# A cross-attention stage written out in 16 steps, with every value product inside its own step and eight places for probabilities

## The reference

```
q = (x @ Wq)        # 2048 rows, 8 heads of 64
k = (context @ Wk)  # 1601 rows
v = (context @ Wv)
scores = einsum('bhnd,bhmd->bhnm', q, k) * 64 ** -0.5
attn = softmax(scores, axis=-1)
out = einsum('bhnm,bhmd->bhnd', attn, v)
x = layernorm(x + out @ Wo + bo)
```

## Time and profile before

| what | us |
|---|---|
| median of 3 runs | 970.12 (964.15, 970.12, 972.71) |
| the profiled execution's own time | 970.8 |
| its span, first to last instruction | 969.0 |
| PE busy | 903.2 (93%) |
| POOL busy | 591.4 (61%) |
| DVE busy | 554.7 (57%) |
| ACT busy | 351.0 (36%) |
| granted TensorE clock, mean | 0.978 |

### The profile page before, as it was taken

One profiled execution on the slowest core, in us unless ns is written; L12 is line 12 of the kernel. 1 busy time (PEld: TensorE's weight loads), 2 busy tenths in 40 slices (PEclk: granted clock), 3 DMA queues, 4 the chain that ended last, 5 costly groups with the idle time before them and its releaser, 6 DMA issues. The chain is left out here.

```text
span 969.0 us, 14096 instructions
## 1 busy us (share of the span) xinstructions
PE 903.2 (93%) x4616; PEld 536.6 (55%) x4616; DVE 554.7 (57%) x1123; ACT 351.0 (36%) x493; POOL 591.4 (61%) x397
## 2 busy tenths in 40 slices
PE   6989699999999999999999999989799999989993
PEld 2655354555465455455445455445478888855552
DVE  3897457568557568557557748653645221235562
ACT  3244144434325444425344425433241211124342
POOL 0463198898777889778789769874104500028885
PEclk9999799999999999999999999989899999999997
DMA  9013300000001000001000001040497100323310
GB/s 281 19 46 111 98 1 1 22 1 1 1 1 45 22 1 2 1 1 44 22 1 1 1 1 44 1 153 1 120 321 260 60 22 22 112 83 109 97 37 17
DMA packets 42877, 52.92 MB, mean 55 GB/s; under 512 B 4400, under 2 KB 33856, under 8 KB 42816
## 3 DMA queue, kind: packets, MB, share of 16 engines
q1 hardware_dynamic: 35808, 44.21, 14.4%
q0 software_dynamic: 3744, 6.32, 2.0%
q10 hardware_dynamic: 3264, 1.57, 0.6%
HBM read 38.42 MB, written 17.59 MB: 58 GB/s over the span
## 5 line engine op out<-in xcount | busy, mean ns | idle before, releaser
L625 POOL TENSOR_TENSOR accG<-accG,probs 128x1024 f32<-128x1024 f32 (+1 forms) x170 | 403.5, 2374 | 39.9 <-ACT probs L658 22.7
L658 ACT ACTIVATE probs<-st 128x1024 f32<-128x1024 f32 (+1 forms) x208 | 211.3, 1025 | 239.1 <-PE st L854 150.3
L712 DVE TENSOR_REDUCE mxp<-mx 128x1 f32<-128x512 f32 x360 | 231.2, 686 | 92.2 <-PE mx L839 89.3
L883 PE MATMUL av<-probs,V 128*64 128x512 f32 (+1 forms) x832 | 192.4, 600 | 0.0
L839 PE MATMUL mx<-K_hi,Q_hi 64*128 64x512 f32 (+1 forms) x480 | 165.4, 404 | 4.7 <-DVE mxp L712 4.7
L854 PE MATMUL st<-Q_hi,K_lo 64*128 64x512 f32 (+1 forms) x416 | 127.0, 408 | 0.0
L854 PE MATMUL st<-M,ones_r 64*128 64x512 f32 (+1 forms) x416 | 123.5, 403 | 0.0
L854 PE MATMUL st<-Q_hi,K_hi 64*128 64x512 f32 (+1 forms) x416 | 98.8, 447 | 12.7 <-ACT probs L658 12.7
L883 PEld LDWEIGHTS av<-probs,V 128*64 128x64 f32 (+1 forms) x832 | 54.1, 136 | 98.2 <-issue 83.0
L839 PEld LDWEIGHTS mx<-K_hi,Q_hi 64*128 64x128 f32 x480 | 76.1, 184 | 53.1 <-DVE mxp L712 28.5
L854 PE MATMUL st<-Q_lo,K_hi 64*128 64x512 f32 (+1 forms) x416 | 86.4, 395 | 0.0
(11 more groups left out here) (198 smaller groups left out, 1240.1 us busy)
## 6 DMA issues: line engine op xcount, KB each, us to landing
w_gate_up<-in_gate_up SPq DMA_DIRECT2D x4, 2048.0 KB, 20.2
w_down<-in_down SPq DMA_DIRECT2D x2, 2048.0 KB, 15.6
xs<-scratch_sorted_x SPq DMA_DIRECT2D x31, 128.5 KB, 2.1
scratch_sorted_x<-zero SPq DMA_DIRECT2D x7, 514.0 KB, 8.0
xT<-in_xT SPq DMA_DIRECT2D x4, 512.0 KB, 8.0
xring<-in_x SPq DMA_DIRECT2D x4, 512.0 KB, 8.6
scratch_x1b<-xT SPq DMA_DIRECT2D x4, 512.0 KB, 2.9
x<-scratch_x1b SPq DMA_DIRECT2D x4, 512.0 KB, 3.9
```

The source lines that it names most:

```text
L625: pool.tensor_tensor(accG[0:r], so_far[0:r], probs[0:r, (p * KT + t) % RING], ALU.add).then_inc(g_add, 1)
L658: act.activation(probs[0:r, s], st[g % 2][0:r, :], ACT.Exp, scale=DH ** -0.5).then_inc(a_probs, 1)
L712: dve.tensor_reduce(mxp[:, par, h * QT + i, j:j + 1], mx[h][:, 0:kn], AX.X, ALU.max).then_inc(v_mx, 1)
L883: mm = pe.matmul(av[h * DH:(h + 1) * DH, :], V[0:r, t, (2 * p + h) * DH:(2 * p + h + 1) * DH], probs[0:r, g % RING, h * QC:(h + 1) * QC], ...
```

## The change

The attention stage is rewritten; the other stages are untouched. On every engine the 16 steps are written out (`for S in range(STEPS)`), and the loops, the counts from registers and the semaphore increments and same-engine waits that served them are gone. What else differs:

- PE takes the tiles in four runs, `RUNS`: tiles 0 to 2, 3 to 5, 6 to 8, 9 to 12. After each run come the values of its own tiles, so all 13 values are in their own step, and tiles 0 and 1 are done whole.
- Where a piece stands in a tile is a table, `PIECE_AT`: for each tile, after how many parts the piece of the first and of the second head comes. Tile 0 has none. The last two pieces stand behind tile 12.
- `sums` of the step before comes after the first run. `accG` is two tensors in turn, so that POOL's first addition waits for the sums of two steps before.
- `RING` is 8. `DIVIDE_AFTER` is (10, 10, 16, 16).
- ACT copies `av` (`copy_av`) ahead of `Q_hi`.

```diff
-DIVIDE_AFTER = (8, 8, 18, 18)
-RING = 4
+RUNS = (range(0, 3), range(3, 6), range(6, 9), range(9, KT))
+PIECE_AT = {1: (4, 4), 2: (4, 4), 3: (0, 2), 4: (1, 3), 5: (3, 4), 6: (0, 2), 7: (1, 3), 8: (3, 4),
+            9: (0, 2), 10: (1, 3), 11: (2, 4), 12: (3, 4)}
+DIVIDE_AFTER = (10, 10, 16, 16)
+RING = 8
...
-        accG = sb("accG", [P, 2 * QC])
+        accG = [sb(f"accG{i}", [P, 2 * QC]) for i in range(2)]
...
+                    if n == 0:
+                        at_least(pool, p_sum, S - 1)
+                        so_far = probs[:, place(S, 0)]
...
+            for S in range(STEPS):
+                c, p = divmod(S, PAIRS)
+                if S > 0:
+                    copy_av(S - 1)
+                if S + 1 < STEPS:
+                    q_high(S + 1)
+                for t in range(KT):
+                    exp(S, t)
+                    if p == 1 and t == NORM_AFTER and c > 0:
+                        norm(c - 1)
...
+                if n > 2:
+                    pe.wait_ge(v_mx, (F - 1) * PIECES + n - 2)
...
+            def tile(S, t, first_piece):
+
+                at_least(pe, a_probs, S * KT + t - 1)
+                for slot in range(4 if first_piece is None else 5):
                     for h in range(2):
-                        score(c, p, t, part, h)
...
+                        if first_piece is None or slot < PIECE_AT[t][h]:
+                            score(S, t, slot, h)
+                        elif slot == PIECE_AT[t][h]:
+                            piece(S + 1, first_piece + h)
+                        else:
+                            score(S, t, slot - 1, h)
...
-            chunk(0, True, False)
-            with pe.Fori(1, CHUNKS - 1) as c:
-                chunk(c, False, False)
-            chunk(CHUNKS - 1, False, True)
-            values(CHUNKS - 1, PAIRS - 1, KT - 1)
+            for S in range(STEPS):
+                c, p = divmod(S, PAIRS)
+                ahead = S + 1 < STEPS
+                max_transpose(S)
+                if ahead:
+                    q_proj(S + 1)
+                n = 1
+                for run in RUNS:
+                    for t in run:
+                        tile(S, t, n if ahead and t in PIECE_AT else None)
+                        n += 2 if t in PIECE_AT else 0
+                    if run is RUNS[0] and S > 0:
+                        sums(S - 1)
+                    if run is RUNS[-1]:
+                        if ahead:
+                            piece(S + 1, n)
+                            piece(S + 1, n + 1)
+                        if p == 0 and c > 0:
+                            output(c - 1)
+                    for t in run:
+                        values(S, t)
             last_output(False)
```

More of the change, by code:

```diff
@@ L523, in rows_of, with place @@
             return P if t < KT - 1 else LAST
[L528 to L540, removed]
+        def place(S, t):
+            return (S * KT + t) % RING
         def piece_of(n):
@@ L551, in _ @@
         def _(sp):
[L552 to L572, removed]
+            x1_tiles = io["x1b"].rearrange("(t p) n -> p t n", p=P)
@@ L609, in inverse @@
                 pool.tensor_tensor(shift3[:], nmean3[:], rstd3[:], ALU.mult).then_inc(g_shift3, 1)
[L611 to L630, removed]
+            for S in range(STEPS):
+                c, p = divmod(S, PAIRS)
+                total = accG[S % 2]
+                shared = LAST_V if S == STEPS - 1 else ()
+                for n, t in enumerate(t for t in range(1, KT) if t not in shared):
+                    if p == 1 and n == 0 and c > 0:
+                        inverse(c - 1)
+                    r = rows_of(t)
+                    pool.wait_ge(a_probs, S * KT + t + 1)
+                    if n == 0:
+                        at_least(pool, p_sum, S - 1)
+                        so_far = probs[:, place(S, 0)]
+                    else:
+                        pool.wait_ge(g_add, S * G_ADDS + n)
+                        so_far = total
+                    pool.tensor_tensor(total[0:r], so_far[0:r], probs[0:r, place(S, t)], ALU.add).then_inc(g_add, 1)
@@ L693, in _ @@
+            copy_av(STEPS - 1)
         @block.vector
         def _(dve):
[L695 to L717 removed]
@@ new lines, in _ @@
+            for i in range(DIVS):
+                divide(STEPS - 2, i)
+            for n, t in enumerate(LAST_V):
+                r = rows_of(t)
+                dve.wait_ge(a_probs, (STEPS - 1) * KT + t + 1)
+                part = probs[0:r, place(STEPS - 1, t)]
+                if n == 0:
+                    dve.tensor_copy(accL[:], part).then_inc(v_add, 1)
+                else:
+                    dve.wait_ge(v_add, n)
+                    dve.tensor_tensor(accL[0:r], accL[0:r], part, ALU.add).then_inc(v_add, 1)
@@ L810, in _ @@
+            for i in range(DIVS):
+                divide(STEPS - 1, i)
             for i in range(QT):
@@ L826, in q_proj, with piece @@
                 mm.then_inc(p_q, 1)
-            def max_scores(F, pair, par, use, n, after=None):
+            def piece(F, n):
                 i, j = piece_of(n)
@@ L984, in _ @@
             last_output(False)
-            sums(CHUNKS - 1, PAIRS - 1, LAST_SUM_USE, shared=True)
+            sums(STEPS - 1)
             last_output(True)
```

381 lines of the change are left out of this document (136 added, 245 removed).

## The result

The changed kernel takes 963.2 us in the median of 6 runs (961.3 to 964.3), the kernel before beside it 969.3 (964.2 to 972.7): a ratio of 0.9931, with an interval of 0.9904 to 0.9957. It is faster by 0.7%, which is inside the range of 960 to 983 and inside "within 1%", but on the other side of zero from the +1.7 us that the sum gave. The profiled execution took 963.4, its span is 961.5, against 970.8 and 969.0.

What follows compares the result with a forecast made beforehand. PE was taken to bound the kernel, busy 32.7 of 33.8 us in an ordinary step. Ordinary steps +2.4, output steps +0.6, first step +1.5, norm +2.7 and last step -5.5 gave +1.7: 972 us, range 960 to 983.

Steps and rivals of the forecast that it cites:

- the closed circle: POOL's additions and PE's sums wait on each other across steps; opening it and dropping loops wins 0.35 a step, 5 us.
- The order run by run: PE's new order in an ordinary step, laid out from pair durations: 34.06 against 33.84, +2.4 us over eleven steps.
- The wait at the last pieces: End of the fourth run: pieces 25 and 26 wait for DVE's reductions 23 and 24, 1.3 us a step.
- The norm: Second step of chunks 1 to 3: value 5 waits for an exponential behind ACT's norm, 0.9 x 3, +2.7 us.
- The first step: First attention step: its runs cost the same excess as the others and it takes in value 12, +1.5 us.
- The last step: Last attention step: no wait of PE for POOL and no fall of the clock, 27.8 against 33.27, -5.5 us.
- POOL: POOL's additions in the new order: begin about 3 us earlier, end about 2 us into the next step, before the sums.
- POOL still decides: Rival: POOL's additions still set the step; ruled out at 30.1 us against 34, no chance of its own.
- The eight places and the second tensor: Ring and sums buffers: two sums tensors open POOL's circle, eight places keep the exponentials from waiting for additions.
- That the waits at the pieces don't show: Rival, 17%: no waits at the last pieces, fourth run 5.9 to 6.1, step 32.9, about 955 us.
- Seams: Rival, 17%: heads out of step at run starts and piece-first tiles lose 0.6 a step, 981 to 984 us.
- The clock in ordinary steps: Rival, 3%: the clock falls in ordinary steps too, 15 x 3 us more, about 1017 us.

Runs made afterwards that it cites:

- The short addition: Kernel before with chunks written out instead of looped, and POOL's addition of tile 12 cut to 16 columns; median 959.6 us, ratio 0.9900.
- the early sums: Changed kernel with, in its last step alone, the sums of the step before behind tile 0 instead of tile 2; 968.6 us, ratio 0.9975.
- the experiment with the small pieces: Changed kernel with the two small pieces (and any output) between values 10 and 11 instead of ahead of value 9; 949.2 us in one run.
- the two copies: The kernel before, unchanged, profiled twice more; 970.3 and 969.0 us.

## Why the prediction came out as it did

**What bounds the kernel, and the closed circle: right.** The short addition gave 0.24 a step, and taking the loops away 0.16 to 0.55 in each of their steps, 4.9 us together in the 14 steps between, where 0.35 each was forecast.

**The order run by run: right in mechanism, 0.44 too long.** A step now, from 320.68 (measured, in brackets as laid out): transpose and projection 1.98 (1.98), first run 4.16 (4.05), sums 0.91 (0.96), values 2.68 and twice 2.72 (2.72), second run 3.93 (4.03), third 3.94 (4.1), fourth 7.00 (7.2), values 3.58 (3.58): 33.62 against 34.06. The terms that were mis-sized are runs two to four. At the end of the second run the change from scores to values was taken as 0.43, from a place where a lone piece stood out of step with its partner. The run ends on an aligned pair, and the change takes 0.33 (PE, same step):

```profile
333.78 0.61 PE L784 MATMUL st<-M,ones_r 64*128 64x512 f32 x2
334.01 0.40 PE L770 MATMUL mx<-K_hi,Q_hi 64*128 64x512 f32 x1
334.34 2.79 PE L806 MATMUL av<-probs,V 128*64 128x512 f32 x12
```

The third ends the same way (341.00 less 340.67); piece 14 in it came 0.1 late, and tile 8's own wait, to 2.58 into the run, covers that. In the fourth, tiles 11 and 12 stood at 2.58 and 3.92 (2.67 and 3.98 laid out), and from piece 25 to the values it took 1.16 instead of 1.24. The errors of the three runs are 0.10, 0.16 and 0.20, against 0.11 the other way in the first, and fourteen times over the step's 0.44 is 6 us. This is the step of the prediction that failed. It forecast +5.7 for the 14 steps between and they gave -0.4.

**The wait at the last pieces: right.** Called 1.3; piece 25 was laid out at 5.96 into the run and came at 5.84, and moving the small pieces away gave 0.93 net of one more change of direction.

**The norm: right.** 0.9 x 3 forecast, 2.8 measured by the norm one tile later.

**Tile 2: right.** No wait for ACT of 0.69 is left in an ordinary step.

**The first step: nearly right, and hidden by the clock.** +1.5 was forecast, +0.3 and +0.5 came in the two profiles of the changed kernel. But the time that this step spends at 0.50 differs between executions, from 5.9 to 8.1 us over all profiles, and it lasts about half a microsecond longer for each of them. At nearly equal stretches, 5.9 us, the kernel before without loops takes 35.57:

```profile
108.53:144.10 35.57, 32.36 (x189) 17.60 (x189) 17.84 (x29) 13.82 (x14) 23.97 (x11) 0.92 0.14 45
```

The changed kernel takes 36.88, which is 1.3 more. With half of the stretch taken off, the seven profiles with the old order in this step give 32.6 to 32.8 and the five with the changed kernel's 33.9 to 34.1: 1.35 more, of which value 12 is 0.9.

**The last step: right.** 27.8 forecast, 27.83 measured, run by run: the first 3.63 (3.46 laid out: tile 2 came 0.16 late), the others 3.46, 3.46 and 4.40 (3.47, 3.47, 4.41). Of the 5.4, the clock is 2.1, the wait 1.9, value 12 in the step before 0.9, the order 0.5. The price of the clock was called 3. And the sums met no wait only by 0.14, which the next point shows: that part was luck.

**POOL: wrong, without harm.** It was said to end 2 us into the next step; it ended 3.75 into it, since ten additions can only follow exponential 3, which in the new order comes 12.3 us into the step (333.00 less 320.68). In the last step that leaves 0.14:

```profile
618.19 25.05 POOL L600 TENSOR_TENSOR accG<-accG,probs 128x1024 f32<-128x1024 f32 x10 [2.18 <-ACT probs L623]
```

It ends at 643.24, and the sums of the last step begin at 643.38. The rival "POOL still decides", which got no chance, was this near to costing what the early sums cost. With a shorter step it does wait, 0.77, as the experiment with the small pieces shows.

**The eight places and the second tensor: credited with opening the circle; they do nothing.** The sum was not touched by it, the account was.

**The rivals.** That the waits at the pieces don't show would have given steps of 32.9. They showed, and steps of 32.7 came only where the pieces were moved. Seams would have made the runs longer than laid out; three of four are shorter. The clock in ordinary steps: 1.00 in all 14. The Trainium skill (TensorE: Matmul & The Clock Gate, "A second HAM failure mode: psum-queue depth-cycling") would have it swing with small waits between groups; no run here shows it, with 0.43 of idle and more at the last pieces of each of the 14 steps between at 1.00.

The profiled execution came 9.2 us below the sum made for it (+1.7 against -7.5 of its span): 6.1 in the steps between, 1.2 in the first step, nearly all of it the shorter spell at half speed, 2.0 outside the 16 steps, where the code is the same but for the last output. That the clock stays up in the last step without the loops, though the wait stays, was not foreseen; for the changed kernel it did not matter, since the wait went as well.

## What to carry to other kernels

A term that repeats many times deserves the row nearest to it in kind, not the most cautious one: 0.1 to 0.2 us in three runs of a step decided the sign of the forecast here. Before a new buffer is credited, ask which event its writer waits for and when that event now comes: here the moved sums did the work, and the second buffer only let POOL begin earlier and wait elsewhere. And look at the last pass apart from the others, since it has less work to hide a late engine: one wait of 1.75 us and the clock behind it were 4 us, more than the fourteen steps between changed together. A stretch that holds a spell at half speed is compared only with one whose spell is as long: the first step's +1.35 showed as +0.3.

## What the runs showed of the hardware that was not expected

A wait of 1.7 to 2.1 us on PE was followed by 3.4 or 6.8 us at a clock of 0.50 in the kernel before (three profiles of three) and in the changed kernel with early sums (one profile), and by none in the kernel before without loops (two of two), where the wait was the same length. Waits of 0.43 to 0.77, among them one in each of the 14 steps between of either kernel, were never followed by one. Every profile shows 0.50 for 5.9 to 8.1 us at the start of the attention, and three executions of one kernel spent 8.1, 6.8 and 8.0 us there.

A hardware loop over a body of four steps cost 2.6 us in its eight steps, 0.16 to 0.55 each. The step ahead of the loop's turn took 34.27 (33.99 and 34.03 in the two copies), the same step of the second pass 33.91 (33.87 and 33.89); written out both take 33.70 to 33.78.

The change from score matmuls to value matmuls took 0.33 where the two heads end together (334.01 to 334.34) and 0.43 where one ends alone (584.64 to 585.07).
